# A two-block graph attention kernel: the first head's counts, masks and weights made tile by tile, a second head and block 1's first attention in another order

## The reference

```python
# x: 256 nodes x 768; src, dst: 4096 edges; self loops are added to both
def gat_conv(x, src, dst, W, a_src, a_dst, b, heads, out_ch):
    h = (x @ W).reshape(n, heads, out_ch)
    e = leaky_relu(einsum('nhc,hc->nh', h, a_src)[src] + einsum('nhc,hc->nh', h, a_dst)[dst], 0.2)
    p = exp(e - segment_max(e, dst)[dst])
    alpha = p / segment_sum(p, dst)[dst]
    return segment_sum(h[src] * alpha[:, :, None], dst).reshape(n, heads * out_ch) + b

# block 0: 8 heads of 768, elu, then one head of 768
h = elu(gat_conv(x, ..., W1, heads=8, out_ch=768)); out = gat_conv(h, ..., W2, heads=1, out_ch=768)
x = layernorm(x + out)
# block 1: 4 heads of 256, then one head of 768, each with a layer norm and a residual product
h = relu(layer_norm(gat_conv(x, ..., W1, heads=4, out_ch=256))) + (x @ Wr1 + br1)
h = layer_norm(gat_conv(h, ..., W2, heads=1, out_ch=768)) + (h @ Wr2 + br2)
x = layernorm(x + h)
```

## Time and profile before

| | us |
|---|---|
| median of 3 runs | 364.79 (364.38 to 365.02) |
| the profiled execution | 364.43 |
| its span in the profile | 362.6 |
| TensorE busy | 349.9 (96%) |
| GpSimd, ScalarE, VectorE busy | 242.5, 218.5, 213.9 |
| mean granted TensorE clock | 0.999 of full speed |

### The profile page before, as it was taken

The page is one execution under the profiler, slowest core; times in us unless marked ns, Lnnn a source line. Parts: engine busy times, 40 slices in busy tenths (PEclk is TensorE's granted clock), DMA queues, the critical chain, the costliest instruction groups (busy, mean ns, idle before and its releaser), DMA issues.

```text
span 362.6 us, 6075 instructions
## 1 busy us (share of the span) xinstructions
PE 349.9 (96%) x2058; PEld 299.1 (82%) x2060; DVE 213.9 (59%) x544; ACT 218.5 (60%) x375; POOL 242.5 (67%) x163
## 2 busy tenths in 40 slices
PE   8999899999999999999999999999999999999994
PEld 4888788888988988988898898898677787788883
DVE  4998864445427327344542832637687767953776
ACT  4995668646745854764775585475476667264601
POOL 2389648784793965779479396574258589687911
PEclk9999999999999999999999999999999999999999
DMA  7988948566646547555664764666072654437002
GB/s 234 302 297 238 398 163 252 183 179 171 198 155 222 163 140 243 162 193 174 174 194 156 217 169 141 251 167 223 5 248 95 209 153 123 161 104 240 6 2 87
DMA packets 24544, 65.15 MB, mean 180 GB/s; under 512 B 1952, under 2 KB 3024, under 8 KB 24528
## 3 DMA queue, kind: packets, MB, share of 16 engines
q1 hardware_dynamic: 20864, 55.02, 46.0%
q10 hardware_dynamic: 3664, 9.92, 10.4%
HBM read 64.15 MB, written 0.79 MB: 179 GB/s over the span
## 4 chain that ended last, share of the span: by engine, by line
PE 78%; DVE 12%; ACT 6%; DMA 2%; issue 1%; ACTq 0%; DVEq 0%
PE ps L985 57%; PE ps L1070 8%; PE ps L1274 5%; PE ps L1104 2%; ACT e L757 1%; DMA b_rows<-in_L_gnn_b 1%; PE ps L1049 1%; DVE e L1491 1%; DVE ps L1544 1%; PE ps L1166 1%; DMA raw<-in_L_gnn_W 1%; ACT ring_hi L357 1%; DVE ps L1554 1%; DVE ps L1628 1%; PE ps L1338 1%
## 5 line engine op out<-in xcount | busy, mean ns | idle before, releaser
L370 POOL TENSOR_TENSOR ring_lo<-raw,ring_hi 128x768 fp32r<-128x768 f32 x92 | 167.0, 1854 | 74.6 <-ACT ring_hi L357 74.6
L357 ACT ACTIVATE ring_hi<-raw 128x768 fp32r<-128x768 f32 x96 | 77.3, 840 | 34.9 <-PE ps L985 28.9
L386 POOL TENSOR_TENSOR ring_lo<-raw,ring_hi 128x512 fp32r<-128x512 f32 (+1 forms) x40 | 59.5, 1519 | 22.5 <-ACT ring_hi L379 22.4
L985 PE MATMUL ps<-ring_hi,zT_hi 128*128 128x256 f32 (+1 forms) x256 | 69.3, 346 | 0.7 <-ACT zT_hi L799 0.7
L985 PE MATMUL ps<-ring_lo,zT_hi 128*128 128x256 f32 (+1 forms) x256 | 67.1, 337 | 0.0
L985 PE MATMUL ps<-ring_hi,zT_lo 128*128 128x256 f32 (+1 forms) x256 | 66.8, 338 | 0.0
L1491 DVE CUSTOM_DVE_ANT_0 e<-ps,att 128x768 f32<-128x768 f32 x38 | 34.3, 957 | 47.5 <-PE ps L985 47.5
L985 PE MATMUL ps<-ring_hi,xT_hi 128*128 128x512 f32 x192 | 51.2, 342 | 0.0
L985 PE MATMUL ps<-ring_lo,xT_hi 128*128 128x512 f32 x192 | 50.0, 336 | 0.0
L985 PE MATMUL ps<-ring_hi,xT_lo 128*128 128x512 f32 x192 | 49.8, 337 | 0.0
L985 PEld LDWEIGHTS ps<-ring_lo,zT_hi 128*128 128x128 f32 x256 | 43.0, 188 | 5.7
(11 more groups left out here) (172 smaller groups left out, 546.9 us busy)
## 6 DMA issues: line engine op xcount, KB each, us to landing
raw<-in_L_gnn_W SPq DMA_DIRECT2D x54, 768.0 KB, 4.5
raw<-in_L_gnn_Wr SPq DMA_DIRECT2D x8, 768.0 KB, 4.3
att<-in_L_gnn_a_src ACTq DMA_DIRECT2D x10, 384.0 KB, 4.0
att<-in_L_gnn_a_dst ACTq DMA_DIRECT2D x10, 384.0 KB, 5.4
raw<-in_L_gnn_W SPq DMA_DIRECT2D x4, 384.0 KB, 5.2
x_sb<-in_x SPq DMA_DIRECT2D x3, 256.0 KB, 5.1
rows_hc<-in_L_gnn_b SPq DMA_DIRECT2D x1, 512.0 KB, 7.9
rows_hc<-in_L_gnn_g SPq DMA_DIRECT2D x1, 512.0 KB, 8.7
```

The costliest lines, as they stand in the source:

```text
L357: eng.activation(slot_hi(c), raw_chunk(c), ACT.Copy).then_inc(hi_done, 1)
L370: eng.tensor_tensor(slot_lo(c), raw_chunk(c), slot_hi(c).bitcast(F32), ALU.subtract)\
L386: eng.tensor_tensor(ring_lo[:, q["ring_at"]:q["ring_at"] + w], raw[:, q["raw_group"], q["raw_at"]:q["raw_at"] + w], ring_hi[:, q["ring_at" ...
L985: last = pe.matmul(ps[:, at + to:at + to + hi - lo], a, b[:, lo:hi], start=start and n == 0 and to != D, stop=stop and n == PASSES - 1, sk ...
```

## The change

In the first head: the copy of the counts' sums (`step_sums`) is moved ahead of `leaks(0)` on ScalarE; VectorE makes the low part of the features of tile 0 alone, begins the counts behind it, and makes that of tile 1 after `normalised`; `counts` and `far` are made in two tiles of 128x256 each and tile 0 goes first in `tile_tops`, `exps` and `normalised`; `am`'s PSUM place changes. TensorE's `weights(0)` stands between the two tiles of the last projecting chunk, two `clear_acc` stand behind the aggregation. The dots of head 1 stand behind `weights_lo(0)`.

In head 1: `scores(1)` waits for the second ELU quadrant of head 0, not the third; ScalarE makes `h_hi` of tile 0 before the last ELU step of head 0, `leaks(1)` between two chunks, and `h_hi` of tile 1 after them; VectorE makes the row tops before the features' low parts. The loop over heads 2 to 7 is not changed.

In block 1, A's scores come before A's second feature part on ScalarE and VectorE, `weigh` follows at once, B's dots come after it; the load of the next attention vectors is started after B's exponentials. `masked_at` of A's tile 0 is moved to bank 5, and TensorE's `weights` waits for the features' low parts, which VectorE did before.

The core of the diff (left out: the function bodies that only change by a parameter, and the counters):

```diff
@@ TensorE
+            def project_chunk(p, h, c, loop=False, at=PROJ, between=None):
                 for i in range(NT):
+                    if between is not None and i == 1:
+                        between()
...
-                project_chunk(1, 1, c)
-            weights(0)
+                project_chunk(1, 1, c, between=(lambda: weights(0)) if c == CH - 1 else None)
...
-            pe.wait_ge(h_lo0_done, NT)
+            aggregate_T(0)
             clear_acc(1)
             clear_acc(2)
-            aggregate_T(0)
...
-                        pe.wait_ge(z_lo_done, 3 * h)
+                        pe.wait_ge(z_lo_done, 3 * h - 1 if first else 3 * h)
                         scores(h)
...
                 if is_gat1(a):
+                    pe.wait_ge(h_lo1_done, 2 * late(a) + 2)
                     pe.wait_ge(p_done, before(a) + 2 * HH)
@@ ScalarE
+            act.wait_ge(counted, 1)
+            act.activation(step_sums, ps[:, STEPS_AT:STEPS_AT + 1 + N], ACT.Copy).then_inc(sums_copied, 1)
             leaks(0)
...
-            act.activation(counts[:, :, :].rearrange("p i n -> p (i n)"), ps[:, COUNT_AT:COUNT_AT + NT * N],
-                           ACT.Copy).then_inc(counts_done, 1)
-            exps(0, (1, 0))
+            counts_tile(1)
+            exps(FIRST_HEAD, (0, 1))
...
-            elu(0)
+            elu(0, between=lambda: projected_after_dots(1, 0))
             split_hi(act, 2, 4)
+            leaks(1)
             split_hi(act, 2, 5)
-            softmax_and_elu(1)
+            projected_after_dots(1, 1)
+            exps(1, (1, 0))
+            after_exps(1)
@@ VectorE, first head
             both_dots(0)
-            for i in range(NT):
-                projected_lo(0, i)
-            dve.wait_ge(h_lo0_done, NT)
-            leaky_scores(0)
+            projected_lo(0, 0)
...
+            dve.wait_ge(h_lo0_done, 1)
+            leaky_scores(FIRST_HEAD)
...
-            for i in (1, 0):
-                tile_tops(0, i)
+            dve.wait_ge(loops_added, NT)
+            far_tile(1)
             dve.wait_ge(counts_done, 1)
-            normalised(0)
+            far_tile(0)
+            dve.wait_ge(far_done, NT)
+            tile_tops(FIRST_HEAD, 0)
+            dve.wait_ge(counts_done, NT)
+            tile_tops(FIRST_HEAD, 1)
+            normalised(FIRST_HEAD, (0, 1))
+            projected_lo(0, 1)
+            weights_lo(0)
             dve.wait_ge(att_loaded, 32 * 2)
-            dots(1, a_s, 0, a_src_done, tiles=(0,))
-            weights_lo(0)
-            dots(1, a_s, 0, a_src_done, tiles=(1,))
+            dots(1, a_s, 0, a_src_done)
             dots(1, a_d, 1, a_dst_done)
             elu(0)
-            softmax(1)
+            dve.wait_ge(z_lo_done, 3)
+            leaky_scores(1)
+            for i in (1, 0):
+                tile_tops(1, i)
+            projected_lo(1, 0)
+            normalised(1)
+            projected_lo(1, 1)
+            weights_lo(1)
@@ VectorE, block 1
             tile_dots(A_GAT1A, 1)
+            masked_scores(A_GAT1A)
             half_lo(A_GAT1A, 1)
-            masked_scores(A_GAT1A)
+            weigh(A_GAT1A, 0)
+            weigh(A_GAT1A, 1)
             tile_dots(A_GAT1B, 0)
-            weigh(A_GAT1A, 0)
+            tile_dots(A_GAT1B, 1)
             half_lo(A_GAT1B, 0)
-            weigh(A_GAT1A, 1)
-            tile_dots(A_GAT1B, 1)
```

More of the change, by code:

```diff
@@ L449, in am_at @@
         def am_at(a, i):
-            at = ACC + (1 + i) * BANK if a is FIRST_HEAD else AM_AT[i]
+            at = (ACC + BANK, T_AT + N)[i] if a is FIRST_HEAD else AM_AT[i]
             return ps[:, at:at + N]
@@ L460, in masked_at @@
                 return am_at(a, i)
-            at = s_at(a, k) + (2 * BANK if i == 0 else 0)
+            at = s_at(a, k)
+            if i == 0:
+                at = 5 * BANK + k * N if a == A_GAT1A else at + 2 * BANK
             return ps[:, at:at + N]
@@ L728, in projected_hi, with projected_after_dots @@
                     projected_tile_hi(h, i)
+            def projected_after_dots(h, i):
+                act.wait_ge(a_dst_done, 2 * h + 2)
+                projected_tile_hi(h, i)
             def projected_tile_hi(h, i):
@@ L778, in weights_tiles_hi, with elu @@
                     act.activation(*weights_tile(a, pT_hi, i), ACT.Copy).then_inc(wt_hi_done, 1)
-            def elu(h):
+            def elu(h, between=None):
                 for q in range(3):
@@ L793, in elu @@
                     act.activation(pair, pair, ACT.Exp, scale=-1.0).then_inc(elu_exp, 1)
+                if between is not None:
+                    between()
                 elu_hi(h, 2)
@@ L812, in softmax_and_elu, with after_exps @@
                 exps(h, (1, 0))
+                after_exps(h, last)
+            def after_exps(h, last=False):
                 att_for(h + 1, last)
@@ L839, in _, with counts_tile @@
                 split_hi(act, 2, c)
-            act.wait_ge(counted, 1)
-            act.activation(step_sums, ps[:, STEPS_AT:STEPS_AT + 1 + N], ACT.Copy).then_inc(sums_copied, 1)
+            def counts_tile(i):
+                act.activation(counts[:, i, :], ps[:, COUNT_AT + i * N:COUNT_AT + (i + 1) * N], ACT.Copy)\
+                   .then_inc(counts_done, 1)
+            act.wait_ge(loops_added, 1)
+            counts_tile(0)
             act.wait_ge(far_done, 1)
-            act.activation(counts[:, :, :].rearrange("p i n -> p (i n)"), ps[:, COUNT_AT:COUNT_AT + NT * N],
-                           ACT.Copy).then_inc(counts_done, 1)
-            exps(0, (1, 0))
+            counts_tile(1)
+            exps(FIRST_HEAD, (0, 1))
             for c in (2, 3):
@@ L918, in _ @@
             x1_scale(1)
+            leaks(A_GAT1A)
             features_hi(A_GAT1A, tiles=(1,))
             chunks_hi(14, 15)
-            leaks(A_GAT1A)
             exps(A_GAT1A, (0, 1))
+            chunks_hi(15, 19)
             features_hi(A_GAT1B, tiles=(0,))
-            chunks_hi(15, 18)
+            chunks_hi(19, 21)
             features_hi(A_GAT1B, tiles=(1,))
             weights_hi(A_GAT1A)
-            chunks_hi(18, 21)
+            leaks(A_GAT1B)
+            exps(A_GAT1B, (0, 1))
             act.wait_ge(a_dst_done, before(A_GAT2))
@@ L931, in _ @@
                    .then_inc(att_loaded, 16)
-            leaks(A_GAT1B)
-            exps(A_GAT1B, (0, 1))
             residual_scale(0, 0)
@@ L1001, in keep_warm @@
                     pe.matmul(ps[:, at:at + BANK], zeros[:, 0:P], zeros[:, :], start=True, stop=True)
-            def project_chunk(p, h, c, loop=False, at=PROJ):
+            def project_chunk(p, h, c, loop=False, at=PROJ, between=None):
                 chunk(p, c)
                 for i in range(NT):
+                    if between is not None and i == 1:
+                        between()
                     by_piece = c == 0 and i == 1 and loop
@@ L1538, in leaky_scores @@
                 if is_gat1(a):
-                    dve.wait_ge(h_lo1_done, 2 * late(a) + 2)
+                    if a == A_GAT1A:
+                        dve.wait_ge(x1T_lo_done, 2 * NT)
+                    else:
+                        dve.wait_ge(h_lo1_done, 2 * late(a) + 2)
                 dve.wait_ge(leak_done, before(a) + NT * n)
@@ L1584, in projected_lo, with normalised @@
                                   ALU.subtract).then_inc(h_lo0_done, 1)
-            def normalised(h):
-                for n, i in enumerate((1, 0)):
+            def normalised(h, order=(1, 0)):
+                for n, i in enumerate(order):
                     dve.wait_ge(e_done, 2 * h + n + 1)
@@ L1659, in _, with far_tile @@
             dve.wait_ge(unpacked, 2)
-            for to, scale in ((in_upper[:, P:N], 2.0 * PACK), (in_lower[:, 0:P], 2.0)):
+            for to, scale in ((in_lower[:, 0:P], 2.0), (in_upper[:, P:N], 2.0 * PACK)):
                 dve.scalar_tensor_tensor(to, ident[:, :], scale, to, ALU.mult, ALU.add).then_inc(loops_added, 1)
-            dve.wait_ge(loops_added, NT)
-            dve.tensor_scalar(far[:, :, :].rearrange("p i n -> p (i n)"), ps[:, COUNT_AT:COUNT_AT + NT * N], 0.0, FAR,
-                              ALU.is_equal, ALU.mult).then_inc(far_done, 1)
+            def far_tile(i):
+                at = COUNT_AT + i * N
+                dve.tensor_scalar(far[:, i, :], ps[:, at:at + N], 0.0, FAR, ALU.is_equal, ALU.mult)\
+                   .then_inc(far_done, 1)
             def softmax_and_elu(h):
```

1 line of the change is left out of this document (removed).

## The result

The changed kernel takes 362.30 us in the median of 10 runs (360.9 to 363.7), the kernel before 364.56 (10 runs); ratio 0.9937, interval 0.9923 to 0.9950. That is faster, by 2.3 us and not by the 4.4 of the sum, and 0.3 above the upper end of the range. The profiled execution took 363.34 with a span of 361.5.

A forecast was written before the change was run, and what follows sets the result against it. TensorE, busy 96% of 362.6 us, bounds the kernel, so only its stops can yield time. Block 0's 2.4 and block 1's 2.05 make 4.4 to 4.5 us, median 360.3; range 359.2 to 362.0 for 8 in 10.

The forecast's parts named there:

- Reading of the stops: TensorE's stops in heads 0 and 1 and block 1, 0.33 to 1.36 us each, are where time can be won.
- First head: Block 0, head 0: first ELU product 1.2 us earlier, at 43.36, limited by VectorE's four dots (bounds 0.9 to 1.8).
- Head 1: Block 0: scores at 48.06, transposes at 54.6; stops of 0.3 and 0.86 us go, the latter with 0.5 margin.
- The loads of phase 3 are started by GpSimd's progress, about a microsecond earlier.: Block 0, head 1's chunks: phase 3's loads start about a microsecond earlier; no cost was given.
- whatever start is won in heads 0 and 1: From 57 to 245 us TensorE has no wait, so starts won earlier move all that follows.
- The prediction's own sign of being wrong: A TensorE wait after 60 us that was not there before, or a stop left at any of the four transposes.
- Block 1: Half A's aggregation 1.2 us closer (bounds 0.8 to 1.36), half B's stop of 0.87 gone (bounds 0 to 0.87).
- the first rival: Block 1 gives only half because ScalarE's queue there is late; gain 2.4 + 1.0, 361.4 us, chance 0.17.
- the first two rivals: Block 1 gives only half, 361.4 us, chance 0.17; or block 0 gives only half, 361.5 us, chance 0.13.
- The fourth: Block 1, rival: load of chunks 18 to 20 lands late ahead of ScalarE's longer queue; slower, up to 366.8, chance 0.03.
- The fifth: Rival: gains are eaten at the loop's head or in block 1's second half; 364.6 us, chance 0.03.
- The split of `far`: First head's counts: two 256-column pieces, 0.76 against 0.69 for one; taken at 0 to 0.15 us.

The follow-up runs named there:

- m: Changed kernel with head 2's attention loads behind `pT_hi` and the last of head 1's four dots behind head 0's first ELU step; 359.69 us, ratio 0.9852.
- f_block0_only: Changed kernel with block 1 as before and head 2's attention loads issued late; 362.62 us, ratio 0.9941 to the kernel before.
- again: The changed kernel unchanged, run and profiled a second time on the chip of later experiments; 362.11 us, ratio 0.9924 to the kernel before.
- b_elu_first: Changed kernel with phase 3's last two chunk roundings behind head 1's whole ELU on ScalarE, attention loads still early; 360.51 us, ratio 0.9876.
- c2_before_att_near: Kernel before, with head 2's attention loads held by a wait until head 1's feature parts are done; 366.05 us, ratio 1.0034.
- c_before_att_early: Kernel before, with head 2's attention loads written behind head 1's feature parts, without a wait; 365.14 us, ratio 1.0004.

## Why the prediction was right or wrong

The direction was right, the size was wrong: 2.3 measured, 4.4 forecast.

*Reading of the stops.* Right. The stops at the scores and at all four groups of transposes stood where the earlier trace rows put them, and none of them was left. The one at the first ELU product stayed, and was forecast to.

*First head.* Right within 0.1: the first ELU product was forecast at 43.36 and came at 43.57 in an execution that was 0.28 late from its start. The limit was VectorE's four dots, as said: with one of them moved (m) the product came 0.66 sooner, each execution taken less its late beginning; the ratios differ by 0.8 us, with an interval of some 0.5 on each.

*Head 1.* The scores were forecast at 48.06 and measured at 48.12, the transposes at 54.6 and 54.66. Less the late start both are 0.2 earlier than forecast, and block 0 gave 2.67 up to the end of head 1 where the sum had 2.4.

*"The loads of phase 3 are started by GpSimd's progress, about a microsecond earlier."* The sentence itself came true (52.4, not 53.4), but here lies the step that failed: the prediction took the load's time to landing as it was, put what follows from it at nothing, and let "whatever start is won in heads 0 and 1" move all that follows. It looked at the weights' load only. It moved head 1's exponentials from 53.89 to 51.0 and did not count what ScalarE issues right behind them, the two attention loads, nor that they thereby pass the weights' load. They cost it 2.5 us of landing time (4.6 to 7.1), ScalarE's ELU of head 1 stood behind the roundings that waited for it, and 1.97 of this reached TensorE in the profiled execution, 1.7 in the second profile. The prediction's own sign of being wrong, a wait of TensorE after 60 us that was not there before, is what came. With the loads put behind, the sum stands: 0.9873 measured, 4.6 us by the ratio and 4.4 by the medians, for 4.4.

*The clock.* Not in the sum. Four of the ten runs of the changed kernel (mean clock 0.992 and 0.993, 363.0 to 363.7) lie above the other six (0.996 and more, 360.9 to 362.7), and the one profile taken among them shows the lower level right behind the stop. That the stop is its cause is not shown, since `f_block0_only` has such executions without it.

*Block 1.* Right: 1.2 and 0.87 were forecast, 1.3 and 0.87 measured. The late queue of ScalarE of the first rival did not come. The measured 362.3 lies near the 361.4 and 361.5 of the first two rivals, but says nothing for them: both blocks gave their whole share.

*Rivals.* The fourth described this mechanism, a load in front of a longer queue of ScalarE, but at the wrong place, in block 1; there the load for chunks 18 to 20 was in time. The fifth named the head of the loop and gave it 0.03. The range ended 0.3 too low, since it held no case in which a load passes another.

*The split of `far`.* The 0.76 that the prediction took from the earlier trace rows for two pieces is that of the leaky scores, another operation. In the changed kernel the two pieces of `far` themselves took 0.76, where the one of 512 columns had taken 0.69, and the transposes still found `am` ready:

```profile
32.60 0.76 DVE L1689 TENSOR_SCALAR far<-ps 128x256 f32<-128x256 f32 x2
```

The Trainium skill (Perfetto Trace Analysis, Optimizing Scalar/DVE Operations) gives each further VectorE instruction on PSUM some 125 ns of access. The trace agrees that two pieces are dearer than one, by 0.07 here. For two added instructions this figure makes 0.25, an estimate, and not the 0.15 to 0.2 that the prediction wrote; in `far` one was added.

## What to carry to other kernels

When a step is moved ahead on an engine that also starts loads, move those loads on paper too, and put their new start beside every other load's: bytes that nobody needs for 20 us (head 2's first dot was at 77.93) can pass bytes that are wanted in four. An engine's queue in which a step on the critical path stands behind a step that waits for a load should be turned round where the load's work is not wanted sooner. And where a stop is won, look for the next stop over the whole stretch behind, since a new one can take back much of what was won (1.97 of 4.8 here).

## What the runs showed of the hardware

- Two loads of 384 KB (one row spread over 128 partitions each), started 0.6 to 1.3 us ahead on ScalarE's queue, brought a load of 768 KB on SyncE's queue from 4.6 to 7.1, 6.8, 6.6 and 7.0 us (changed kernel, again, `b_elu_first`, `c2_before_att_near`), and the next load, in the kernels with late attention loads, to 8.4 to 9.4. Started 3.4 us ahead or 2.7 behind they cost it nothing measurable (4.6 in `c_before_att_early`, 4.8 in m).
- Most of the delay lies ahead of the first packet: it comes 1.0 us behind the load's start with nothing in front, 2.8 in the changed kernel. The Trainium skill (DMA: Bandwidth & Descriptors, Queues, rings and completion order) has each DMA engine take turns, packet by packet, between the queues that it has work for. With its usual delay the weights' load would have had packets from 53.4 or so on, in turn with the others; this trace has none before 55.2. Whether the engines had its packets and did not take them, or did not have them yet, no trace here shows.
- A sequencer starts a load ahead of the engine's queued activations: in `c_before_att_early` the loads stood behind the leaks and the feature parts of head 1 in the text, and the first started at 50.72, before these ran (50.82 and 51.54). With a wait on a semaphore in front of them (`c2_before_att_near`) the first started at 53.5, when the feature parts were done.
- After a stop of 1.8 us (idle) the granted clock was 0.51 for 3.4 us in one profile, the lower level of 1.2 GHz; after one of 1.53 and one of 2.12 in two others it stayed at 1.00. Executions with a lower mean clock were four of ten and none of six with the stop of the changed kernel, six of twelve with the one of about 2 us, none of five with 0.6 us, but also four of twelve without a stop (`f_block0_only`) and two of 22 of the kernel before beside it. What decides between them stays open.
